# A fused attention and expert kernel: weight fetches two steps ahead, zero-fills over fewer steps, scatters and gathers dealt out anew

## What is computed

```python
def _L0_xattn_ref(x, latents, ...):          # x: the context, latents: the normalised input
    xn = _layernorm(x, gamma_media, beta_media)
    ln = _layernorm(latents, gamma_lat, beta_lat)
    q = ln @ Wq + bq
    kv = jnp.concatenate([xn, ln], axis=1) @ Wkv + bkv
    ...
    attn = jax.nn.softmax(jnp.einsum('bhid,bhjd->bhij', q * DH ** (-0.5), k), axis=-1)
    return jnp.einsum('bhij,bhjd->bhid', attn, v)... @ Wo + bo

def _L0_ffn_ref(x, Wr, br, W1, b1, W2, b2):
    probs = jax.nn.softmax(jnp.einsum('bsh,he->bse', x, Wr) + br, axis=-1)
    top_p, top_i = jax.lax.top_k(probs, 2)
    ...
    h = jax.nn.relu(jnp.einsum('bsh,ehd->bsed', x, W1) + b1)
    y = jnp.einsum('bsed,edh->bseh', h, W2) + b2
    return jnp.einsum('bseh,bse->bsh', y, cw)

x = x + jnp.tanh(g_xattn[0]) * _L0_xattn_ref(ctx_1024, _layernorm(x), ...)
x = x + jnp.tanh(g_ffn[0]) * _L0_ffn_ref(_layernorm(x), ...)
```

## Time and profile before

| | us |
|---|---|
| median of three runs | 800.37 |
| lowest, highest | 799.6, 803.32 |
| profiled execution, its own time | 800.92 |
| profiled execution, its span | 799.2 |
| PE busy in it | 757.6 (95%) |
| DVE, ACT, POOL busy | 523.1, 492.8, 428.3 |

### The profile page before, as it was taken

The page is one execution under the profiler, slowest core; times in us unless marked ns, Lnnn a source line. Parts: engine busy times, 40 slices in busy tenths (PEclk is TensorE's granted clock), DMA queues, the critical chain, the costliest instruction groups (busy, mean ns, idle before and its releaser), DMA issues.

```text
span 799.2 us, 17227 instructions
## 1 busy us (share of the span) xinstructions
PE 757.6 (95%) x5306; PEld 634.3 (79%) x5306; DVE 523.1 (65%) x1814; ACT 492.8 (62%) x1615; POOL 428.3 (54%) x443
## 2 busy tenths in 40 slices
PE   7999999999899999999999999999999889879995
PEld 7778777777788787888877888878987768778774
DVE  5636677685858566575869687686758566375545
ACT  4676777776766466565767665766656665554331
POOL 2233365646543535434578665686654686444573
PEclk9999999999999999999999999999999999999998
DMA  6836162644776836463214556274731145543132
GB/s 189 247 146 219 60 238 73 231 161 144 246 265 230 298 127 229 165 199 110 57 37 148 190 172 219 66 213 156 238 117 31 47 136 182 179 115 105 53 89 83
DMA packets 122109, 124.10 MB, mean 155 GB/s; under 512 B 14857, under 2 KB 87842, under 8 KB 122018
## 3 DMA queue, kind: packets, MB, share of 16 engines
q1 hardware_dynamic: 113920, 108.16, 40.8%
q0 software_dynamic: 7168, 14.69, 6.5%
q10 hardware_dynamic: 930, 0.15, 0.1%
HBM read 33.52 MB, written 53.28 MB: 109 GB/s over the span
## 4 chain that ended last, share of the span: by engine, by line
PE 73%; DVE 7%; POOL 6%; issue 6%; ACT 4%; DMA 2%; SPq 1%; ACTq 0%; POOLq 0%; DVEq 0%
PE shared L1500 12%; PE batch L1451 11%; PE batch L1438 10%; PE hid_ps L1361 7%; PE xy_ps L1375 6%; PE batch L1446 5%; PE shared L1284 4%; PE shared L1286 3%; PE shared L1285 3%; ACT probs L798 2%; POOL qT L718 2%; PE xy_ps L1338 2%; POOL yg L718 2%; POOL probs L728 1%; PE batch L1428 1%
## 5 line engine op out<-in xcount | busy, mean ns | idle before, releaser
L728 POOL TENSOR_TENSOR probs<-probs,rsums 128x512 f32<-128x512 f32 x128 | 132.9, 1038 | 244.2 <-DVE rsums L1214 243.6
L798 ACT ACTIVATE probs<-batch,neg_max 128x128 f32<-128x128 f32 x512 | 180.4, 373 | 2.1 <-DVE neg_max L1218 2.1
L878 ACT ACTIVATE qT<-shared,tb 128x512 f32<-128x512 f32 x128 | 87.3, 695 | 96.4 <-PE shared L1286 96.3
L1451 PE MATMUL batch<-pT_sb,kvn 128*128 128x512 f32 x256 | 133.8, 604 | 4.7 <-ACT pT_sb L806 4.7
L1438 PE MATMUL batch<-kvT,qT 128*128 128x128 f32 x1024 | 136.4, 276 | 0.8 <-ACT qT L878 0.8
L704 POOL DMA_INDIRECT sorted<-xn,row_of x112 | 114.8, 1025 | 26.8 <-issue 26.8
L1438 PEld LDWEIGHTS batch<-kvT,qT 128*128 128x128 f32 x1024 | 125.3, 193 | 1.2 <-ACT qT L878 1.2
L1500 PE MATMUL shared<-M,oT 128*128 128x128 f32 x1024 | 125.2, 276 | 0.2
L1500 PEld LDWEIGHTS shared<-M,oT 128*128 128x128 f32 x1024 | 119.5, 192 | 1.1 <-issue 1.1
L1214 DVE RECIPROCAL rsums<-sums 128x4 f32<-128x4 f32 x128 | 23.2, 181 | 137.0 <-ACT probs L798 135.6
L798 ACT ACTIVATION_READ_ACCUMULATOR probs<-batch,neg_max 128x1 f32 x512 | 109.9, 215 | 0.0
(11 more groups left out here) (187 smaller groups left out, 1252.2 us busy)
## 6 DMA issues: line engine op xcount, KB each, us to landing
wt<-wall SPq DMA_DIRECT2D x110, 321.0 KB, 3.2
sorted<-yg SPq DMA_DIRECT2D x63, 512.0 KB, 4.5
xt<-sorted SPq DMA_DIRECT2D x133, 64.0 KB
sorted<-y_sb SPq DMA_DIRECT2D x133, 64.0 KB
kv<-in_ctx_dram SPq DMA_DIRECT2D x16, 256.0 KB
kv<-in_x_dram SPq DMA_DIRECT2D x16, 256.0 KB
xres<-in_x_dram SPq DMA_DIRECT2D x32, 128.0 KB, 2.3
out_dram<-x SPq DMA_DIRECT2D x15, 256.0 KB
```

The lines of the kernel that those rows point to most:

```text
L728: nc.gpsimd.tensor_tensor(pv, pv, rsums[:, m % 2, :].unsqueeze(2).broadcast_to([P, 4, P]), ALU.mult).then_inc(probs_ready, 1)
L798: last = nc.scalar.activation(probs[:, m % 2, c * P:(c + 1) * P], batch_ps[m % BANKS][:, c * P:(c + 1) * P], ACT.Exp, bias=neg_max[:, m % ...
L878: nc.scalar.activation(qT[:, g % 2, :, number, :], sh[:, :].rearrange("p (b i) -> p b i", b=GB), ACT.Identity, bias=tb[:, number:number + ...
L1451: nc.tensor.matmul(batch_ps[m % BANKS][:, :], kvn[:, m % KVN, :], pT_sb[:, :], start=True, stop=True).then_inc(o_ready, 1)
```

## The change

It has four parts.

- **Weights.** SP fetches the weights of the tile at step n in step n − 2, not n − 1. For the tiles that ACT serves, the table read and its waits go to the end of ACT's step n − 2 (`read_experts`); the copies stay. In steps from 131 on the routing exponential comes after the copies of its step.
- **Clearing.** The 63 zero-fills are spread over steps 1 to 44.
- **Scatters.** One scatter in s = 2, two in 3, two in 4, one in 5, two in 6.
- **Gathers.** Rooms are smaller while attention runs, with one more in some places if the step has a tile; from 131 on a tile step has room for one, for two in every fourth step, and each dense step for three. As worked out by the plan's own functions, the gathers stand thus:

| steps | before | after |
|---|---|---|
| 73 to 130 | 60 | 47 |
| 131 to 142 | 12 | 15 |
| 143 on | 40 (two in each, three from 151) | 50 (three in each, two in step 159) |
| first sum of groups 0 to 13 in step | 83, 91, 98, 106, 112, 123, 131, 137, 144, 148, 152, 155, 158, 158 | 88, 96, 106, 115, 128, 134, 141, 145, 148, 150, 153, 156, 158, 159 |
| last step | 160 | 161 |

```diff
-SCATTER = (2, 3, 4, 6)
+SCATTER = (2, 3, 3, 4, 4, 5, 6, 6)
...
-CLEARING = 56
+CLEARING = 44
...
-GATHERS = {0: 3, 1: 2, 5: 2, 7: 2}
+GATHERS = {0: 2, 1: 1, 5: 1, 7: 1}
+BESIDE_TILE = {1: 1, 5: 1, 7: 1}
...
                 if n >= TAIL:
-                    room = 2 + (n >= DENSE_SLOT[E]) if n in DENSE_AT else 1
+                    room = 3 if n in DENSE_AT else 1 + (TILE_AT[n] % 4 == 3) if n in TILE_AT else 4
                 else:
-                    room = GATHERS.get(n % GB, 0)
+                    room = GATHERS.get(n % GB, 0) + (BESIDE_TILE.get(n % GB, 0) if n in TILE_AT else 0)
...
-                if TILE_AT.get(n + 1, N_TILES) < LATE:
-                    fetch_weights(TILE_AT[n + 1])
+                if TILE_AT.get(n + 2, N_TILES) < LATE:
+                    fetch_weights(TILE_AT[n + 2])
...
-            def scatter_rows(g, c):
-
-                k = CHUNK_OF_GROUP[g]
-                if c == 0:
+            def scatter_rows(g, c, choice):
+
+                if c == 0 and choice == 0:
                     pool.wait_ge(placed, g + 1)
                     pool.wait_ge(cleared[g], cleared_before(g))
-                for choice in range(2):
-                    nc.gpsimd.indirect_dma_start(sorted_rows[k][:, :], bass.IndirectOffsetOnAxis(ap=row_of[:, g, choice, c:c + 1], axis=0),
-                                                 xn[:, g % 2, c, :], None).then_inc(scattered[g % 2], 16)
+                nc.gpsimd.indirect_dma_start(sorted_rows[CHUNK_OF_GROUP[g]][:, :],
+                                             bass.IndirectOffsetOnAxis(ap=row_of[:, g, choice, c:c + 1], axis=0),
+                                             xn[:, g % 2, c, :], None).then_inc(scattered[g % 2], 16)
...
-                if s in SCATTER and 0 <= g < SORTED:
-                    scatter_rows(g, SCATTER.index(s))
+                for part in range(2 * 4):
+                    if s == SCATTER[part] and 0 <= g < SORTED:
+                        scatter_rows(g, part // 2, part % 2)
...
-                g = n // GB - 1
-                if n % GB == 6 and 0 <= g < G:
-                    act.wait_ge(route_step, routed(g) + 2)
-                    nc.scalar.activation(prob[:, :, :], shift[:, :, :], ACT.Exp).then_inc(rexp_done, 1)
+                if n < TAIL:
+                    route_exponentials(n)
...
+                if n >= TAIL:
+                    route_exponentials(n)
+                if TILE_AT.get(n + 2, 0) >= LATE:
+                    read_experts(TILE_AT[n + 2])
+
+            def route_exponentials(n):
+
+                g = n // GB - 1
+                if n % GB == 6 and 0 <= g < G:
+                    act.wait_ge(route_step, routed(g) + 2)
+                    nc.scalar.activation(prob[:, :, :], shift[:, :, :], ACT.Exp).then_inc(rexp_done, 1)
...
-            def fetch_weights(i):
+            def read_experts(i):
 
                 if i == LATE:
                     act.wait_ge(experts_ready, 1)
...
                 if i == LATE or reads_table(i):
                     experts.clear()
                     read_table(mybir.EngineType.Activation, 1, experts, i, N_TILES, E - 1)
+
+            def fetch_weights(i):
+
                 wait(act, y_done, i - WB + 1)
```

## The result

The changed kernel takes **793.16 us** (median of 4 runs, 791.88 to 794.23) beside 801.85 for the kernel before (4 runs, 799.6 to 805.14): a ratio of 0.9888, 95% interval 0.9846 to 0.9930. The forecast was 794.6 with a range of 790 to 801. The profiled execution of after took 793.38 us with a span of 791.6, against 800.92 and 799.2: 7.6 us less span where 5.8 were forecast.

A forecast was written before the change was run, and what follows sets the result against it. Three limits: PE with small holes in attention, a PE, ACT and DVE chain in the tiles alone, POOL's gather queue at the end. Gains of 12.3 us less 6.5 took the median from 800.37 to 794.6 us, range 790 to 801.

The forecast's parts named there:

- Weights: First tile matmuls of steps 43, 51, 59: fetching weights one step earlier closes three PE holes, 5.3 us gained.
- Clearing: Attention steps: zero-fills over 44 steps help the same holes at step 51, with longer early bursts; costed at nothing.
- Scatters: Steps 18 to 19 and 26 to 27: one scatter fewer on POOL closes holes of 0.53 and 0.29, 0.8 us gained.
- Gathers and sums: Steps 80-81 gain 1.0 us, 120-123 1.8, 112-114 1.9; sums moved into 88-89 cost 0.5, block 96-99 nothing.
- The tiles alone: Hole of 1.68 us at step 130 gives 1.5, turned-tile wait of 3.19 gives 0.5, DVE late next; 2.0 gained.
- The dense steps: From step 143: ten more gathers put the last 7.5 us later, one DVE block fewer gives 1.0 back; net +6.5.
- The sum: Whole kernel: 12.3 us gained ahead of step 143 less 6.5 lost in dense steps, 5.8 us less.
- The signs named beforehand: Tile waits at 43, 51, 59 gone; PE busy 112-114; dense gathers from near 721 to 783, gapless; three DVE blocks.
- signs of being wrong: Other-named holes at the same tiles; row-count waits over 1.1 us at 89, 97; DVE later at step 135; POOL gaps.
- gathers are hidden: Dense steps: PE's 16 steps of 3.5 us set the end, ten gathers cost nothing, 788.1 us; chance 0.05.
- The rival in which the gaps form anew: Attention and tiles: only the weights' holes close, 6.8 us, less 6.5 in the dense steps, 800.1 us; chance 0.27.
- The slower rival: Dense phase: POOL full from 733 us outweighs early gains under 2.5 us, slower than 804.4, example 806; chance 0.11.

The follow-up runs named there:

- the improved kernel: Two gathers in each tile step from 131 and sums of groups 0 and 1 moved to steps 90 and 98, against the changed kernel: 781.66 us, ratio 0.9761.
- the experiment above: Sum of group 5 taken in step 136 instead of 134, against the improved kernel, which showed the 3.67 us; repeated on another chip: 779.75 us, ratio 0.9718.
- the kernel with group 5's sum moved (first run): Sum of group 5 taken in step 136 instead of 134, against the improved kernel, on the chip with the stretches: 805.09 us, ratio 0.9932.
- the other two kernels: Scatters in pairs again, against the improved kernel: 809.65 us; gather part with two per tile step from 131, against the kernel before: 816.81 us.

## Why the prediction was right, point by point

**Weights: right in size, partly wrong in cause.** 5.82 us for 5.3. For the tile of step 59 I said that SP waits for the normalised rows ahead of the fetch. The order of SP's queue shows that as only a part: the clears of steps 55 and 56 stood there too, and taking these away alone closed that hole (step 59 to 4.71 us). For step 51 I named the read of the table; that read of 3.79 us, the longest of the earlier trace rows, takes 1.69 when no clears stand ahead of it, and then that hole is closed too. That the fetch comes too late for all these tiles was right: one step earlier, it closes every one of them.

**Clearing: costed at nothing, worth 4.2 us alone and about nothing in company.** The sum was right because it counted the holes once, with the weights. That the clears helped "the same holes" stood in the text, and no price for them alone.

**Scatters: 0.60 us for 0.8 in the two places named**, and the rest missed. In the improved kernel the part brings over 2 us, half of it in steps 123 and 124. The parts measured alone, 7.0 (weights and clearing), 4.2 (gathers) and −1.4 (scatters), make 9.8 us where the change gives 12.15; the missing 2.3 are the loss at step 59 in the profile of the scatters alone, a place that the weights close in the changed kernel.

**Gathers and sums: right in the sums, in one place by luck.** 0.93 for 1.0 in steps 80 to 87, 1.93 for 1.9 in steps 112 and 113. For steps 121 to 124 it is 2.01 for 1.8, but the 1.8 were all put down to the gathers. These alone give 0.87 there, and the scatters alone 0.86, for which the prediction had nothing. The moved sums of steps 88 to 90 were charged 0.5 us and came out 0.23 to the good: steps 88 and 89 lengthen by 1.52 together, and step 90, which lost its sum, shortens by 1.75. At steps 96 to 99 the wait of 1.10 us stands where the prediction put it, and the block still gains 0.67. The text named the groups wrongly: counted as in the code from 0, the sums that go to steps 88 and 96 are those of groups 0 and 1, and the one that leaves step 112 goes to step 128. Steps and prices were the right ones.

**The tiles alone: 1.2 us for 2.0.** The hole of 1.68 us closes, and the wait of 3.19 is 2.30 for DVE's activations, the cause that was named as late next. That would be 2.6. But PE then runs some 3 us at the lower clock of 1.2 GHz (granted clock 0.58 from 701.70 to 704.70). PE in order of time at that place of after:

```profile
701.78 1.75 PE L1388 MATMUL batch<-wt,hs 128*128 128x128 f32 x8 [2.30 <-DVE hs L1238]
703.32 0.64 PE L1351 MATMUL batch<-ident,xt 128*128 128x128 f32 x2
703.74 1.92 PE L1374 MATMUL hid_ps<-xtT,wt 128*128 128x128 f32 x8
705.45 1.12 PE L1388 MATMUL batch<-wt,hs 128*128 128x128 f32 x8
```

3.67 us from the first to the last of them, as in the experiment above, so 1.56 more than at the full clock. 2.6 − 1.6 = 1.0, and 1.19 were measured. The prediction had no term for the clock: in before the longer wait of 3.19 us was followed by a matmul row of 1.16 us. A profile of another kernel shows what the stage takes without it: with the weights and the clearing alone there is a wait of 3.09 us for ACT at this place and no fall of the clock, and from the row maximum of step 127 to the first dense matmul it is 49.15 us, against 52.01 in before and 50.82 in after. And ACT's part, credited with 0.5 us, gives nothing that can be measured.

**The dense steps: +5.5 us for +6.5.** 50 gathers take 782.22 − 719.95 = 62.27 us, 1.271 each, which is 7.0 us more than before (forecast 7.5). Behind the last gather come three blocks and not four, and the first starts 2.50 us after its issue where it was 2.96: 6.10 falls to 4.60 us, 1.5 back where 1.0 was forecast. 7.0 − 1.5 = 5.5.

**The sum.** Ahead of the dense steps 12.3 us were forecast, and the first dense gather is 13.1 earlier; 13.1 − 5.5 = 7.6. The 1.8 us beyond the forecast are four misses that partly cancel: 1.85 more in the attention steps, 0.8 less in the tiles alone, 1.0 less paid in the dense steps, and step 8 reached 0.25 later. The signs named beforehand are there: the first dense gather near 721 (719.95), the last near 783 (782.22), no gap on POOL between them, three blocks of DVE behind. Of the signs of being wrong one is there, the wait for row counts at step 97 (1.10 us), but not the one at step 89; a gap of another name at a tile stands at step 135. The rival "gathers are hidden" fell: POOL spends 0.95 us of its own time on each gather, 50 times. The Trainium skill, DMA: Bandwidth & Descriptors, section "Anatomy of one DMA — SWDGE (gpsimd) path", calls the time for descriptor generation small; these rows speak against it for such gathers. The rival in which the gaps form anew fell too; its dense cost was real. It describes the gather part alone, which ends at the time of before. The slower rival needed the early stages to give less than 2.5 us, and they gave 13.1. What the prediction did not see is that its two largest terms belong to different edits: the one line for the weights gave the whole gain (ratio 0.9872 alone, 0.9888 for the change), and the gather plan alone paid for itself and no more (1.0004).

## What to carry to other kernels

Where an engine's queue ends the program, count the operations that a plan leaves for that queue before you thin them out earlier: ten gathers moved behind the last tile cost 5.5 us, and putting nine of them beside the tiles, where POOL was half idle, gave 8 to 9 us back (7.7 by the spans, 9.1 by the medians). Edits that close the same hole do not add up, and an edit whose gain can't be told alone may show it in company, so measure a part both on the old kernel and in the new one. After each closed wait read what is late next at the same place: here moving one sum two steps took 1.05 us off a wait, and 2.6 off an execution in which the clock had fallen behind it. Before you lay a lost microsecond to an edit, look at the granted clock in that stretch.

## What the runs showed of the hardware

**A wait may cost more than its length.** Behind waits of 2.24, 2.25, 2.30, 2.50 and 2.90 us at step 135 the next eight matmuls took from 1.63 to 1.91 us where 1.06 is usual; behind 3.12 and 3.27 us (the scatters alone, the weights alone) the clock fell one matmul row later. The granted clock is 0.53 to 0.62 in the 3 us windows of these seven kernels, and 1.56 us are lost where it was worked out. Behind 3.19 us in before, 3.09 with the weights and the clearing, and 2.48 with the gathers alone it stayed at 1.00 and the matmuls took 1.16. At step 59 it fell behind 1.87 us, in one profile. The length of the wait alone does not decide it in these rows, and the clock differs between executions of one program: the ten with the gathers alone have mean granted clocks from 0.983 to 0.994 and take from 806.23 down to 800.43 us. What decides it was not settled.

**Stretches in which all engines stand still.** In the three kernels that ran together on one chip, pauses of some 2 us came back behind step 125, and never in the attention steps. POOL in the kernel with group 5's sum moved (first run):

```profile
743.00 0.95 POOL L721 DMA_INDIRECT qT<-sorted,row_of  x1 [2.17 <-PE batch L1426]
...
756.26 0.95 POOL L721 DMA_INDIRECT yg<-sorted,row_of  x1 [2.21 <-remote]
...
769.54 0.96 POOL L721 DMA_INDIRECT yg<-sorted,row_of  x1 [2.10 <-PE batch L1426]
...
782.77 0.96 POOL L721 DMA_INDIRECT qT<-sorted,row_of  x1 [2.07 <-PE shared L1426]
```

DVE waits in the same stretches for something that the profile calls remote (7.94 us at 782.55). They lie 13.2 to 13.3 us apart, and in the other two kernels they stand 4.5 and 11.8 us later, which is by how much longer these kernels' spans are (808.9 and 816.2 for 804.4): in these three profiles they are tied to places of the program. The same kernel on another chip has none of them and is 25 us faster; the kernel before, of which no profile was taken on that chip, took 811.37 us there and 801 to 803 elsewhere. Their cause stays open; for the method it means that a kernel is compared only with runs of before on the same chip, and that even the ratio (0.9932 there, 0.9718 on the other chip) can carry the chip.
